# The third corner of five taps scaled on ScalarE, and added on VectorE in one piece, in a four-layer image kernel

## The reference

```
x = x + attention(gn(x))            # L0: scores of 4096 x 4096, softmax
x = x + involution(gn(x))           # L1: weights by position, 3x3, dilation 2
x = x + mlp_after_7x7(gn(x))        # L2: depthwise 7x7, layernorm, 128-512-128 MLP
x = x + deformable_conv(gn(x))      # L3: 9 taps, each sampled at 4 corners
```

```
val[p, k, :] = sum over corners q = 0..3 of w4[p, q, k] * patch[p, k, q, :]
```

## Time and profile before

| | us |
|---|---|
| median of 3 runs | 4000.69 |
| the profiled execution, its own time | 4003.65 |
| its span, first to last instruction | 4001.9 |
| PE busy | 3438.6 |
| DVE busy | 3275.3 |
| POOL busy | 2429.2 |
| ACT busy | 2182.4 |

### The profile page before, as it was taken

The page is one execution under the profiler, slowest core; times in us unless marked ns, Lnnn a source line. Parts: engine busy times, 40 slices in busy tenths (PEclk is TensorE's granted clock), DMA queues, the critical chain, the costliest instruction groups (busy, mean ns, idle before and its releaser), DMA issues. The chain is left out here.

```text
span 4001.9 us, 81119 instructions
## 1 busy us (share of the span) xinstructions
PE 3438.6 (86%) x29499; PEld 2151.7 (54%) x29499; DVE 3275.3 (82%) x6755; ACT 2182.4 (55%) x4937; POOL 2429.2 (61%) x2656
## 2 busy tenths in 40 slices
PE   4999988989999988989999998988999998993555
PEld 1666633446666653336666663345666673343444
DVE  4999877679999967759999968858999987855666
ACT  2444423358788852338888862346887883232333
POOL 3455552458778843438778845338877865336775
PEclk9999999999999999999999999999999999995665
DMA  1000002155555512055555521044554530227775
GB/s 51 10 12 12 28 18 52 60 155 153 147 158 144 152 39 51 1 171 146 156 145 153 151 74 43 19 132 140 151 156 143 157 111 19 50 83 208 221 217 176
DMA packets 219947, 426.99 MB, mean 107 GB/s; under 512 B 27825, under 2 KB 126540, under 8 KB 217512
## 3 DMA queue, kind: packets, MB, share of 16 engines
q0 software_dynamic: 92160, 302.06, 26.2%
q1 hardware_dynamic: 127346, 119.80, 10.5%
q10 hardware_dynamic: 54, 0.01, 0.0%
HBM read 340.97 MB, written 60.71 MB: 100 GB/s over the span
## 5 line engine op out<-in xcount | busy, mean ns | idle before, releaser
L1804 POOL TENSOR_TENSOR xl<-pt 128x192 bf16<-128x192 f32 (+1 forms) x1024 | 694.3, 679 | 419.5 <-ACT pt L956 287.6
L956 ACT ACTIVATE pt<-bank 128x512 f32<-128x512 f32 x1024 | 607.3, 593 | 333.4 <-DVE bank L1361 219.3
L597 PEld LDWEIGHTS bank<-vt,pt 128*128 128x128 bf16 x8192 | 549.3, 98 | 244.6 <-ACT pt L956 6.7
L1793 POOL DMA_INDIRECT G<-patch_table,idx x576 | 578.2, 1004 | 167.7 <-issue 112.2
L1293 DVE TENSOR_REDUCE mxc<-bank 128x1 f32<-128x512 f32 x896 | 607.9, 680 | 39.6 <-PE bank L520 37.0
L597 PE MATMUL bank<-vt,pt 128*128 128x129 bf16 (+1 forms) x8192 | 634.4, 220 | 1.1 <-ACT osb L964 1.1
L1353 DVE TENSOR_TENSOR xl<-pt 128x320 bf16<-128x320 f32 (+1 forms) x1024 | 513.4, 502 | 57.9 <-PE bank L597 32.1
L597 PE MATMUL bank<-vt,xl 128*128 128x129 bf16 x4096 | 401.8, 221 | 21.3 <-DVE xl L1353 19.3
L520 PE MATMUL bank<-reg,qh 128*128 128x512 bf16 x896 | 343.1, 384 | 17.5 <-DVE mxc L1293 13.6
L1529 DVE SCALAR_TENSOR_TENSOR G<-xn,vec,G 128x512 f32<-128x512 f32 x384 | 305.0, 832 | 24.8 <-issue 20.3
L559 PE MATMUL bank<-qh,reg 128*128 128x512 bf16 x768 | 294.4, 383 | 28.3 <-ACT bank L947 21.7
(11 more groups left out here) (295 smaller groups left out, 7231.0 us busy)
## 6 DMA issues: line engine op xcount, KB each, us to landing
patch_table<-valt SPq DMA_DIRECT2D x64, 512.0 KB, 7.1
G<-patch_table,idx POOLq DMA_INDIRECT x576
x_cur<-in_x SPq DMA_DIRECT2D x4, 2048.0 KB, 8.3
xl<-in_x SPq DMA_DIRECT2D x32, 256.0 KB
attn_out<-ob SPq DMA_DIRECT2D x32, 256.0 KB, 2.9
x_store<-x_cur SPq DMA_DIRECT2D x4, 2048.0 KB, 6.5
xr<-x_store SPq DMA_DIRECT2D x32, 256.0 KB, 4.9
out<-fo SPq DMA_DIRECT2D x32, 256.0 KB
```

Source lines behind the costliest of these rows:

```text
L597: last = mm(O[t // 2][:, c0:c0 + width], image[:, at % ring, t * 128:(t + 1) * 128], vhl[:, values, st, 0:width], start=(st == 0 and part ...
L956: A(pt[:, at % PT_RING, :], ST[at % ST_RING] if n else ST_FIRST[at % 3], ACT.Exp, scale=SCALE).then_inc(s["exp_done"], 1)
L1793: g.indirect_dma_start(out=patches(j, k), out_offset=None, in_=table[:], in_offset=bass.IndirectOffsetOnAxis(ap=idx[:, j * K1 + k:j * K1 + ...
L1804: g.tensor_tensor(pl[:, at % PL_RING, 0:stop], pt[:, at % PT_RING, 0:stop], ph[:, at % PT_RING, 0:stop], ALU.subtract).then_inc(s["pl_p"], 1)
```

## The change

A constant `ACT_THIRD = 5` is added. On ACT, `second_corner` scales, for taps 0 to 4, corner 2 of the patch in place as well, right behind corner 1 of the same tap: six operations in step +4, five in step +5, three in step +6. On DVE, `interpolate` does corner 3 of all nine taps first (+3 to +5), then a drain and corner 2 of taps 5 to 8 alone, two in +6 and two in +7; +8 has none. The five scaled corners are added in +9, behind the addition of corner 1, after one more drain, in one TENSOR_TENSOR of 128 x 640. The tail is not touched.

```diff
+ACT_THIRD = 5
...
                     last = A(src, src, ACT.Copy, scale=w4[:, j, K1 + k:K1 + k + 1])
+                    if k < ACT_THIRD:
+                        src = patches(j, k)[:, 2 * C:3 * C]
+                        last = A(src, src, ACT.Copy, scale=w4[:, j, 2 * K1 + k:2 * K1 + k + 1])
...
                 if r < SPT - 1:
-                    for o in range(3 * r, 3 * r + 3):
-                        corner, k = 2 + o // K1, o % K1
-                        if corner > 2 and k == 0:
-                            dve.drain()
+                    if r == 3:
+                        dve.drain()
+                    last_taps = range(ACT_THIRD + 2 * (r - 3), min(ACT_THIRD + 2 * (r - 2), K1))
+                    for corner, k in ([(3, k) for k in range(3 * r, 3 * r + 3)] if r < 3
+                                      else [(2, k) for k in last_taps]):
...
                         v.tensor_tensor(dst, dst, patches(j, joint)[:, C:2 * C], ALU.add)
                     dve.drain()
+                    dst = val[:, j % 2, 0:ACT_THIRD, :]
+                    v.tensor_tensor(dst, dst, held[:, 0:ACT_THIRD, 2 * C:3 * C], ALU.add)
+                    dve.drain()
                     dve.sem_inc(s["val_rdy"], 1)
```

## The result

The changed kernel takes 4017.49 us, the median of 6 runs (4014.74 to 4020.26), against 4003.01 us for the kernel before beside it (6 runs). The ratio is 1.0035, with a 95% interval of 1.0022 to 1.0048: 14 us slower. The forecast was 3948, and its range ended at 3992. It was wrong in sign.

What follows compares the result with a forecast made beforehand. DVE was taken to set the pace at 17.4 us a tile; -0.65 on DVE and +0.10 for ACT gave 0.55 less, 53 us over 96 tiles, so 3951 in the profiled execution, 3948 as median; range 3900 to 3992.

Steps and rivals of the forecast that it cites:

- What bounds the kernel: Attention with sampling: DVE sets the pace with about 17.2 us of work in a tile of 17.4.
- The removed operations: Five single-tap additions leave DVE (L1330), saving 1.32 to 1.79 us a tile.
- The added addition: One DVE addition of 128 x 640, 822 ns, with its drain 0.91 us a tile.
- a net of -0.65: DVE's work per tile, removal and addition together: middle of -0.88 to -0.41 us.
- The rival of conserved waiting: POOL's L1804 blocks DVE's next operation instead; 0.31 us a tile saved, 3971 us; chance 0.19.
- What hides the lump is ACT's lead: Steps +4 and +5: a 1.2 us lead nearly covers 1.3 us of need; 0.1 us a tile of new waiting.
- The rival on the slower side: ACT becomes the bound at L559 behind the preload in +4 and +5: 0.4 us a tile more, about 4039; chance 0.10.
- ACT was early at L987: Argument against the slower case: ACT waited there for PE, 31.6 us in 450.
- The wait at L612: PE's wait for val_rdy (L611 before the change) was to go from 0.91 to 0.4 to 0.6 us a tile.
- ACT's busy share: In a middle stretch after the change, ACT was to be busy 88 to 92%.
- three signs of being wrong: ACT busier than DVE, L559's wait past 1.5 us a tile, or L611 waiting as long as before.
- The step of 2.25 us: In a middle stretch a step was to last about 2.25 us in place of 2.32.

Runs made afterwards that it cites:

- e12: Changed kernel without ScalarE's five added scalings and without the addition of 128 x 640; 3929.78 us, ratio 0.9820 to the kernel before.
- e10: Changed kernel with the five third-corner scalings one by one in ScalarE's steps +1, +2, +3, +7 and +8; 3989.56 us, ratio 0.9966.
- e13: Changed kernel without ScalarE's five scalings, the 128 x 640 addition replaced in place, ahead of val_rdy, by a one-input maximum; 3966.76 us, ratio 0.9914.
- e14: Changed kernel without ScalarE's five scalings, the addition replaced by a one-input maximum of 128 x 640 right behind val_rdy; 3953.85 us, ratio 0.9874.
- e15: Changed kernel without ScalarE's five scalings, the addition replaced by a one-input maximum of 128 x 640 in step +8; 3950.54 us, ratio 0.9872.
- e4: Changed kernel with the five third-corner scalings moved to ScalarE's steps +6 (one), +7 (two) and +8 (two); 3997.18 us, ratio 0.9988.

## Why the prediction was wrong, step by step

- **What bounds the kernel.** Right: the stretches, the step of 2.32 us, VectorE as the engine that set the pace, 15.5 us of TensorE's work in a tile (in 350 us of e12, where `val_rdy` is hardly waited for, a tile takes 16.4 us, and 15.7 without the four waits). What was missing is how much such a lead of VectorE is worth: taking away 1.3 to 1.8 us of its work brought 72 / 96 = 0.75 us, for then the preload's 0.5 to 0.6 us a tile is what remains.
- **The removed operations.** 1.32 to 1.79 us of work, worth 0.75 of time. Mis-sized: I took work off the leading engine as time off the tile, one for one.
- **The added addition.** Its duration was right, 822 ns forecast and 824 measured as minimum. Its price was not: I entered it at 0.91 in a net of -0.65. It costs 0.54 of time (52 / 96), so the net is 20 / 96 = 0.21 in place of 0.65. Both terms came out smaller than entered, but the addition takes back 72% of what the removal gives and not 58%. Of its 52 us, 15 are what it costs more than an equally long maximum in the same place; that this is collision with GpSimd is argued, not shown. The rival of conserved waiting pointed there but priced only the removed side.
- **What hides the lump is ACT's lead.** This is the step that turned the sign. I valued the lead at 1.2 us against a need of 1.3 and left 0.1 us a tile. Measured on top of VectorE's half: 35 / 96 = 0.36. TensorE's wait at the preload grew by 0.95 us a tile (0.51 to 1.46) where I put 0.10. The lead was often not there: the 0.51 us that I read at L559 lies for the most part behind +4 to +6, so in many tiles ScalarE was already late in the second corner's steps before the change, and every scaling more could only add to that. My sum also took a mean step of TensorE, 2.2 us; beside +4 and +5 stand its steps with transposes or with neither, 1.89 and 1.55 in my own rows. Where 0.29 us more lies in a step that has idle time, it costs little, 8 us for all five (e10).
- **The rival on the slower side** named the place, L559 behind the preload, rightly, and the rest of the waits less so: `val_rdy` fell to 0.32 us a tile and the two together gave +14 us, not +38. It had a chance of 0.10, on the argument that ACT was early at L987. That argument was of no use: the lead at L987 was consumed by the lump (31.6 us of waiting became 7.5), and at the preload there was often none.
- **The wait at L612** was to fall to 0.4 to 0.6; it fell to 0.32. With VectorE's half alone it is 0.83, so the fall is mostly TensorE coming later to L612, behind the preload.
- **ACT's busy share** was forecast at 88 to 92% and is 88; a share under 90% hid a wait of 1.46 us a tile. In the 450 us none of my three signs of being wrong shows: ACT is just less busy than DVE (398 against 404 us), the wait at L560 just under 1.5, and L612 waits less. Over the three attentions from end to end the first two do: ACT 1533 against DVE 1510 us, and 145.4 / 96 = 1.51. The step of 2.25 us (it is 450 / 193 = 2.33) and DVE at 93 to 96% (it is 90%) failed in the 450 us too.

The differences between the runs, in a row: -72 us for the removal, +52 for the addition, +28 for the lump, +8 for ScalarE's added work, +16 in all. They close on the measured 14 by construction, since each is the step from one median to the next; they say how the change divides, and don't test it.

Open is why three taps do no better than five, whether even single taps on VectorE cost 8 to 9 us by their place or by the drain, and how much of the addition's price is collision.

## What to carry to other kernels

Before moving work to an engine "with a fifth of its time free", find in its own list what the bounding engine waits for, and count how much stands ahead of it in that one step: the free time counts only in the step in which it lies, and small pieces belong in the steps that show idle time. If the bounding engine already waits there, the lead is gone before the change. Price a change on two sides by running each half alone, since a delay from one side hides the other's. And when small operations are merged into a long one with two SBUF inputs beside a busy GpSimd, don't take its undisturbed duration for its price: an equally long operation with one input was 15 to 33 us cheaper here.

## What the runs showed of the hardware

An operation on VectorE with one SBUF input, a maximum over 128 x 640 float32, took 820 to 824 ns in each tile of e13, e14 and e15, beside a GpSimd that reads SBUF, while an addition of 128 x 640 with two inputs, 824 ns at the least, took up to 1434 (in e4). Put into the same step the addition made the whole kernel 33 us slower than the maximum did.
